# Routing tables of a mixture-of-experts kernel rebuilt: ranks, a scan, token numbers in the one-hots, and the last low parts on another engine

## The chip, the cores and the metric

The kernel runs on one core of a Trainium2 chip. Its time is the device time of one execution in microseconds (us). The engines run side by side and wait for each other by semaphores: TensorE (PE) multiplies, VectorE (DVE), ScalarE (ACT) and GpSimd (POOL) do the rest, SyncE (SP) issues plain DMAs. GpSimd issues the indirect DMAs that gather and scatter rows.

## The reference, cut to what matters

All is fp32; T = 2048 tokens of 512 numbers, 8 experts, 2 chosen for each token.

```python
x = x + xattn(ctx, ctx, mask, kpad, layernorm(x), Wq, bq, Wk, bk)   # softmax(scores * layernorm(x))
xn = layernorm(x).reshape(-1, 512)
shared = silu(xn @ shared_gate_w) * (xn @ shared_up_w) @ shared_down_w
logits = xn @ router_w                                # (2048, 8)
top_val, top_idx = top_k(logits, 2)
probs = zeros.at[arange(T)[:, None], top_idx].set(sigmoid(top_val))
for e in range(8):                                    # probs is 0 where e is not chosen
    gate, up = split((probs[:, e, None] * xn) @ gate_up_w[e], 2)
    shared += (silu(gate) * up) @ down_w[e]
out = x + shared
```

## The kernel before, in words

The tokens are 16 tiles of 128 (`TILES`). In a first phase (to about 122 us) each tile passes attention, normalisation, router logits and the shared expert. In a last phase (from about 153 us) come 39 routed jobs (`ROUTED`), numbered 16 to 54: each gathers 128 rows of one expert from memory (`gather`, `xg`), transposes them, multiplies by that expert's weights and adds the result to the output by an indirect DMA (`scatter`). Rows beyond a job's tokens go to a spare place. Jobs are sorted by expert.

Between the phases stands the routing, on which the change works. `fetch` copies logits from PSUM, first of 14 tiles (`FIRST`), then of the last two. `choose` finds a maximum by a chain: maximum, equality, index, one-hot `oh`, and the first choice masked out before the second. `ohs` is their sum. TensorE's `ranks` gives by matrix products with `ones` and `triangle` each choice's number within its expert. `count` turns them into jobs per expert (`ntile`, a running sum by three shifted additions) and `base`, `place_of_choice` into a `slot` for each of the 32 columns of choices, of which `job` and `row` are the high and low bits. `G` is the one-hot of the job, `OB` that of the row, in four parts that share two buffers. TensorE's `job_rows` multiplies them to a map job by row that holds a token number, in two halves (`R`: the token's number in its tile, and 128 times the tile, made by ScalarE from `G`), to be added. `jgather` and `jscatter` are the row numbers for the DMAs, `jexpert` the experts of the jobs, `jneed` how far each scatter waits for earlier ones.

Weights and activations are split in a high part and a low part (`gu_hi`, `gu_lo`; `x_hi`, `x_lo`), and three products stand for an fp32 one. Expert weights come in 27 chunks (`CHUNKS`): SyncE loads one into `stage`, ScalarE makes the high part, GpSimd the low part (`low_part`, `late_low`). The last six chunks come late, since their places hold other tensors in the first phase.

The order on each engine is the order in which the code is written; each engine has one queue, and nothing is moved by a scheduler. `then` makes VectorE wait for the end of its own instruction. `keep_busy` are transposes whose result is not used. On GpSimd a gather waits until `xg` is free (`h_s`), a scatter until y is there and until the three scatters before it are done, as far as they may touch the same rows; the first seven wait for all three.

## Time and profile before

| | before |
|---|---|
| median of 3 runs | 353.49 us (353.42 to 355.19) |
| profiled execution | 353.46 us |
| its span | 351.6 us |
| TensorE busy | 318.0 us, 90% |
| VectorE busy | 206.8 us, 59% |
| ScalarE busy | 181.0 us, 51% |
| GpSimd busy | 212.2 us, 60% |
| mean granted TensorE clock | 0.981 |
| moved by DMA | 50.60 MB, mean 144 GB/s |

Rows of the profile are of one execution; L numbers are lines of the kernel. Of each instruction it shows start and duration. Instructions of one engine overlap a little, so the distance of two starts is less than a duration where nothing is waited for. PE is TensorE's matrix product, PEld its weight load.

### The profile page before, as it was taken

Reading aid. Unit: us, or ns where it says so; the run is one execution under the profiler, and the core shown is the slowest. Engines: PE = TensorE matmul, PEld = TensorE weight load, DVE = VectorE, ACT = ScalarE, POOL = GpSimd, SP = SyncE. Lnnn points to the kernel's source line nnn. Section 1 sums busy time; section 2 is a strip of 40 time slices with the busy share of each in tenths; the row PEclk is TensorE's granted clock in tenths of the full one; section 3 lists DMA queues with packets and bytes.
Section 4 is the critical chain, followed back from the end, with each engine's and each line's share of the span. In section 5 each row is a group of like instructions: output and inputs, shape, how many; then the busy total and the mean of one; then the engine's idle time right before and its main releaser. Section 6 shows DMA issues by size and latency. Waiting matters only on the chain.

```text
span 351.6 us, 6597 instructions
## 1 busy us (share of the span) xinstructions
PE 318.0 (90%) x1677; PEld 222.4 (63%) x1677; DVE 206.8 (59%) x453; ACT 181.0 (51%) x409; POOL 212.2 (60%) x206
## 2 busy tenths in 40 slices
PE   2868999899999897879998989999999999999990
PEld 1334666676777666647766757777777777777760
DVE  0695888899998799834443444444444444445440
ACT  2578777767868745135544434444344444434430
POOL 0699999988686700393683666665465565555333
PEclk9989999999999999699999999999999999999998
DMA  7956678856755421281556486666666576565635
GB/s 175 320 216 230 213 239 241 245 204 209 236 159 187 170 92 7 66 292 38 90 97 115 70 170 99 109 110 118 117 122 108 88 128 108 115 123 100 113 45 75
DMA packets 29762, 50.60 MB, mean 144 GB/s; under 512 B 5472, under 2 KB 9312, under 8 KB 29728
## 3 DMA queue, kind: packets, MB, share of 16 engines
q0 software_dynamic: 9008, 21.66, 34.4%
q1 hardware_dynamic: 19232, 27.99, 24.7%
q10 hardware_dynamic: 1488, 0.54, 0.7%
q8 instruction: 16, 0.26, 0.3%
q14 instruction: 18, 0.15, 0.1%
HBM read 30.45 MB, written 19.73 MB: 143 GB/s over the span
## 4 chain that ended last, share of the span: by engine, by line
PE 60%; POOL 12%; DMA 10%; issue 9%; DVE 4%; SPq 2%; ACT 2%; POOLq 0%; DVEq 0%; ACTq 0%
PE bank L963 10%; PE bank L1007 10%; PE bank L968 8%; DMA out_rows<-y,jscatter 6%; PE bank L1028 4%; PE bank L1034 4%; PE bank L1031 4%; POOL gu_lo L362 4%; PE bank L1133 4%; PE bank L1016 2%; POOL dn_lo L362 2%; DMA xin<-in_x 2%; PE bank L926 2%; PE bank L985 2%; PE bank L935 2%
## 5 line engine op out<-in xcount | busy, mean ns | idle before, releaser
L442 POOL DMA_INDIRECT out_rows<-y,jscatter x39 | 61.9, 1587 | 74.1 <-DMA out_rows<-y,jscatter 52.1
L1007 PE MATMUL bank<-gu_hi,x_lo 128*128 (+1 forms) x220 | 72.8, 452 | 0.6 <-DVE x_lo L679 0.6
L963 PE MATMUL bank<-gu_hi,x_hi 128*128 (+1 forms) x220 | 61.6, 402 | 3.7 <-ACT x_hi L514 2.6
L423 POOL DMA_INDIRECT xg<-xn_rows,jgather x39 | 41.7, 1069 | 27.5 <-DVE jgather L839 15.3
L1007 PEld LDWEIGHTS bank<-gu_hi,x_lo 128*128 128x128 f32 x220 | 41.3, 189 | 18.0 <-issue 4.3
L878 DVE SCALAR_TENSOR_TENSOR h<-bank,xg,h 128x256 f32<-128x256 f32 x39 | 18.9, 484 | 56.0 <-ACT h L603 56.0
L522 ACT CAST h_hi<-bank 128x256 fp32r<-128x256 f32 x55 | 20.5, 374 | 60.7 <-PE bank L1016 57.0
L963 PEld LDWEIGHTS bank<-gu_hi,x_hi 128*128 128x128 f32 x220 | 40.0, 188 | 14.7 <-issue 2.8
L679 DVE TENSOR_TENSOR x_lo<-bank,x_hi 128x512 fp32r<-128x512 f32 x55 | 37.9, 690 | 19.0 <-ACT x_bf L515 18.6
L362 POOL TENSOR_TENSOR gu_lo<-stage,gu_hi 128x1024 bf16<-128x1024 f32 x18 | 43.4, 2410 | 5.6 <-ACT gu_hi L501 5.6
L603 ACT ACTIVATE h<-bank,xg 128x256 f32<-128x256 f32 x39 | 18.5, 474 | 50.0 <-PE bank L1007 26.4
L968 PE MATMUL bank<-gu_lo,x_bf 128*128 (+1 forms) x172 | 44.2, 379 | 0.0
L685 DVE TENSOR_TENSOR h_lo<-bank,h_hi 128x256 fp32r<-128x256 f32 x55 | 23.1, 420 | 32.9 <-ACT h_bf L523 32.8
L1034 PE MATMUL bank<-dn_hi,h_lo 128*128 (+1 forms) x86 | 35.5, 494 | 0.0
L514 ACT CAST x_hi<-bank 128x512 fp32r<-128x512 f32 x55 | 31.9, 581 | 6.3 <-PE bank L1133 4.3
L515 ACT CAST x_bf<-bank 128x512 bf16<-128x512 f32 x55 | 32.9, 598 | 0.0
L1028 PE MATMUL bank<-dn_hi,h_hi 128*128 (+1 forms) x86 | 30.8, 439 | 2.1 <-DVE x L699 1.0
L887 DVE COPY y<-bank 128x512 f32<-128x512 f32 x39 | 26.6, 681 | 1.3 <-PE bank L1034 1.3
L1031 PE MATMUL bank<-dn_lo,h_bf 128*128 (+1 forms) x86 | 26.5, 391 | 0.0
L1133 PE MATMUL bank<-ident,xg 128*128 128x128 f32 x156 | 23.5, 273 | 2.2 <-DMA xg<-xn_rows,jgather 2.2
L357 POOL TENSOR_TENSOR pen<-mask_pen,kpad_pen 128x512 bf16<-128x512 bf16 x16 | 18.6, 1160 | 10.1 <-DVE kpad_pen L705 10.0
L362 POOL TENSOR_TENSOR dn_lo<-stage,dn_hi 128x1024 bf16<-128x1024 f32 x9 | 21.9, 2438 | 4.5 <-ACT dn_hi L501 4.4
(145 smaller groups left out, 553.2 us busy)
## 6 DMA issues: line engine op xcount, KB each, us to landing
stage<-in_L_ffn_gate_up_w SPq DMA_DIRECT2D x16, 512.0 KB, 3.9
xin<-in_x SPq DMA_DIRECT2D x16, 256.0 KB, 4.4
xn_rows<-xn SPq DMA_DIRECT2D x16, 256.0 KB, 4.0
stage<-in_L_ffn_down_w SPq DMA_DIRECT2D x8, 512.0 KB, 3.7
out_rows<-x SPq DMA_DIRECT2D x16, 256.0 KB, 4.3
out_rows<-zeros POOLq DMA_DIRECT2D x1, 1024.0 KB, 5.0
ctx_in<-in_ctx SPq DMA_DIRECT2D x1, 768.0 KB, 8.8
xg<-xn_rows,jgather POOLq DMA_INDIRECT x39
```

Of the source, the lines that this page charges most:

```text
L362: g.tensor_tensor(third((gu_lo, dn_lo), c), stage[:, c % 3], third((gu_hi, dn_hi), c).bitcast(f32), ALU.subtract).then_inc(lo_s, 1)
L423: g.indirect_dma_start(out=xg[:, r, :], out_offset=None, in_=xn_dram, in_offset=bass.IndirectOffsetOnAxis(ap=jgather[:, n - TILES:n - TILE ...
L442: g.indirect_dma_start(out=out, out_offset=bass.IndirectOffsetOnAxis(ap=jscatter[:, n - TILES:n - TILES + 1], axis=0), in_=y[:, r, :], in_ ...
L515: a.copy(x_bf[:, n % TS], rows_T(n)).then_inc(xbf_s, 1)
L679: v.tensor_tensor(x_lo[:, n % TS], rows_T(n), x_hi[:, n % TS].bitcast(f32), ALU.subtract).then_inc(xlo_s, 1)
L963: tn.matmul(ps_g(n)[:], x_hi[:, n % TS, k, :], gu_hi[:, e, k, :], start=(k == 0), stop=False)
L968: tn.matmul(ps_g(n)[:], x_bf[:, n % TS, k, :], gu_lo[:, e, k, :], start=False, stop=False)
L1007: last = tn.matmul(ps_g(n)[:], x_lo[:, n % TS, k, :], gu_hi[:, e, k, :], start=False, stop=(k == KC - 1))
L1028: tn.matmul(ps_y(n)[:], h_hi[:, n % 2, c, :], dn_hi[:, e, c, :], start=(c == 0), stop=False)
L1031: tn.matmul(ps_y(n)[:], h_bf[:, n % 2, c, :], dn_lo[:, e, c, :], start=False, stop=False)
L1034: last = tn.matmul(ps_y(n)[:], h_lo[:, n % 2, c, :], dn_hi[:, e, c, :], start=False, stop=(c == IC - 1))
L1133: last = tn.transpose(ps_xT[n % 2][:, k * P:(k + 1) * P], xg[:, n % XS, k * P:(k + 1) * P], ident[:])
```

## The change

- `choose_both` finds both choices of the last two tiles by counting: a logit's rank is the number of logits that are larger, or as large and of a lower expert (`below`); rank 0 and 1 are the choices. The 14 tiles before keep the chain.
- The running sum in `count` is one `tensor_tensor_scan`.
- `OB` carries the token number: 32 instructions of 128 elements compare with the row and multiply by `tokens`, in fp16 and in a buffer of their own; `R`, `tok1` and ScalarE's multiplications and copy go. The map has one half, 39 columns, and `jgather` and `jscatter` read it from PSUM.
- `last_normal` moves ahead of `fetch`; `job_experts` moves behind the shared gates; the down product of tile 13 moves behind the map; `h_transpose` of tile 15 gets a PSUM bank of its own and moves ahead of the down product of tile 14.
- The low parts of chunks 24 to 26 are made by VectorE (`last_low`), one before the routed jobs and one in each of jobs 18 and 19.
- On GpSimd the gather runs five jobs ahead of the scatter, where it was four.

```diff
@@ -32,13 +32,14 @@
 READY = EARLY + 1
+LAST = CHUNKS - 3
 FIRST = TILES - LAG
@@ -373,9 +377,8 @@ (GpSimd)
             def late_low(c):
-                place, i = c // 3, c % 3
-                if i < 2:
-                    t = TILES - XS + 2 * (place - 7) + i
+                if c % 3 < 2:
+                    t = TILES - XS + c % 3
...
-            for c in range(READY, READY + 3):
+            for c in range(READY, LAST):
                 late_low(c)
...
+            gather(TILES + XS)
             for n in range(TILES, JOBS):
-                if n + XS < JOBS:
-                    gather(n + XS)
+                if n + XS + 1 < JOBS:
+                    gather(n + XS + 1)
                 scatter(n)
-                if n in (TILES + 1, TILES + 2):
-                    late_low(READY + 3 + n - TILES - 1)
@@ -586,15 +590,8 @@ (ScalarE)
-            act.wait_ge(G_s, 1)
-            for t in range(TILES):
-                last = a.mul(R[:].rearrange("p (k t) m j -> p k t m j", k=K)[:, :, t, 1, :],
-                             G[:].rearrange("p (k t) j -> p k t j", k=K)[:, :, t, :], float(P * t))
...
+            act.wait_ge(map_ps, 4)
             late_high(EARLY + 3)
-            act.wait_ge(map_ps, 4)
-            a.copy(amap[:].rearrange("p a j -> p (a j)"), ps_map).then_inc(map_s, 1)
@@ -768,11 +765,31 @@ (VectorE)
+            def choose_both(first, end):
+                n = end - first
+                src = lgs[:, first:end, :]
+                seen = src.unsqueeze(2).to_broadcast([P, n, E, E])
+                own = src.unsqueeze(3).to_broadcast([P, n, E, E])
+                v.tensor_tensor(larger[:], seen, own, ALU.is_gt)
+                then(v.tensor_tensor(as_large[:], seen, own, ALU.is_ge))
+                then(v.tensor_tensor(as_large[:], as_large[:], below[:].unsqueeze(1).to_broadcast([P, n, E, E]), ALU.mult))
+                then(v.tensor_tensor(larger[:], larger[:], as_large[:], ALU.max))
+                then(v.tensor_reduce(eq[:, first:end, :], larger[:], X, ALU.add))
+                v.tensor_scalar(ohs[:, (first + 1) * E:(end + 1) * E].rearrange("p (t e) -> p t e", e=E),
+                                eq[:, first:end, :], float(K), None, ALU.is_lt).then_inc(ohs_s, 1)
+                for k in range(K):
+                    v.tensor_scalar(oh[:, k].rearrange("p (t e) -> p t e", e=E)[:, first:end, :], eq[:, first:end, :],
+                                    float(k), None, ALU.is_equal).then_inc(oh_s, 1)
...
-                for i, d in enumerate((1, 2, 4)):
-                    then(v.tensor_tensor(ntile[i + 1][:, 4:], ntile[i][:, 4:], ntile[i][:, 4 - d:4 - d + E], ALU.add))
-                then(v.tensor_tensor(base[:], ntile[3][:, 4:], ntile[0][:, 4:], ALU.subtract))
+                then(v.tensor_tensor_scan(base[:], ones[:, 0:E], ntile[:, 3:3 + E], 0.0, ALU.mult, ALU.add))
...
-                dve.wait_ge(G_s, 1)
-                v.tensor_scalar(R[:, :, 0, :], G[:], tok1[:], None, ALU.mult).then_inc(R1_s, 1)
 
             def row_of_choice(part):
-                n = NC // 4
-                if part >= 2:
-                    dve.wait_ge(map_ps, part - 1)
                 dve.wait_ge(row_s, 1)
-                v.tensor_tensor(OB[part % 2][:], iotap[:].unsqueeze(1).to_broadcast([P, n, P]),
-                                wide(rowf[:, part * n:(part + 1) * n], [P, n, P]), ALU.is_equal).then_inc(OB_s, 1)
+                for i in range(part * NC // 4, (part + 1) * NC // 4):
+                    last = v.tensor_scalar(OB[:, i, :], iotap[:], rowf[:, i:i + 1], tokens[:, i:i + 1], ALU.is_equal, ALU.mult)
+                last.then_inc(OB_s, 1)
...
+            def rows_to_gather():
+                dve.wait_ge(map_ps, 4)
+                v.tensor_scalar(jgather[:], ps_map, -1.0, 0.0, ALU.add, ALU.max).then_inc(table_s, 1)
...
+            def last_low(c):
+                if c % 3 < 2:
+                    t = TILES - 2 + c % 3
+                    dve.wait_ge(st_xn[t % XS], stored_xn(t))
+                    dve.wait_ge(xT_ps, t + 1)
+                else:
+                    dve.wait_ge(max_s, TILES)
+                dve.wait_ge(hi_s, c + 1)
+                v.tensor_tensor(third((gu_lo, dn_lo), c), stage[:, c % 3], third((gu_hi, dn_hi), c).bitcast(f32),
+                                ALU.subtract).then_inc(lolast_s, 1)
+
+            last_normal()
+            x_low(TILES - 2)
             fetch(0, 0, FIRST)
-            x_low(TILES - 2)
-            last_normal()
             choose(0, 0, FIRST)
-            h_low(FIRST - 1)
             x_low(TILES - 1)
             choose(1, 0, FIRST)
+            clear_ends()
+            sum_of_choices(0, FIRST)
             fetch(1, FIRST, TILES)
-            choose(0, FIRST, TILES)
-            choose(1, FIRST, TILES)
-            chosen_sum()
+            choose_both(FIRST, TILES)
             weights_of_choices()
             count()
             place_of_choice()
             job_of_choice()
-            row_of_choice(0)
-            row_of_choice(1)
-            row_of_choice(2)
-            row_of_choice(3)
-            job_experts()
-            tables()
+            for part in range(4):
+                row_of_choice(part)
+            rows_to_gather()
+            h_low(FIRST - 1)
             gated_shared(TILES - 2)
+            rows_to_scatter()
             gated_shared(TILES - 1)
             y_shared(FIRST - 2)
+            job_experts()
             h_low(TILES - 2)
-            scatter_waits()
             y_shared(FIRST - 1)
             h_low(TILES - 1)
+            scatter_waits()
+            last_low(LAST)
             y_shared(TILES - 2)
             y_shared(TILES - 1)
...
                 if n > TILES:
                     h_low(n - 1)
+                if n in (TILES + 2, TILES + 3):
+                    last_low(LAST + n - TILES - 1)
                 gated(n)
@@ -1096,29 +1125,28 @@ (TensorE)
             h_transpose(FIRST - 1)
+            xn_transpose(TILES - 1)
             gate_up_high(TILES - 2, SHARED)
-            xn_transpose(TILES - 1)
...
             gate_up_high(TILES - 1, SHARED)
-            down(FIRST - 1, SHARED)
             pe.wait_ge(pexp_s, TILES)
             ranks()
             gate_up_low(TILES - 1, SHARED)
             gate_up_rest(TILES - 1, SHARED)
-            keep_busy(28)
-            pe.wait_ge(R1_s, 1)
+            keep_busy(20)
+            pe.wait_ge(G_s, 1)
             for part in range(4):
-                pe.wait_ge(R0_s, min(part + 1, 2))
                 job_rows(part)
-                keep_busy(4)
-            keep_busy(6)
+                keep_busy(5)
+            down(FIRST - 1, SHARED)
             h_transpose(TILES - 2)
+            pe.wait_ge(scatter_s, 1)
+            h_transpose(TILES - 1)
             down(TILES - 2, SHARED)
-            h_transpose(TILES - 1)
             down(TILES - 1, SHARED)
```

VectorE from the cast of `row` on, before. `OB` are the row one-hots, their number a buffer, `ecmp` to `jlow` the experts:

```order
L807 CAST rowf<-row 128x32 [waits dve_step]
L810 TENSOR_TENSOR G<-jobf,jcolb 128x1248
L813 TENSOR_SCALAR R<-G,tok_101 128x32x39 [waits G_s]
L820 TENSOR_TENSOR OB_91<-iotap,rowf 128x1024 [waits row_s]
L820 TENSOR_TENSOR OB_92<-iotap,rowf 128x1024 [waits row_s]
L820 TENSOR_TENSOR OB_91<-iotap,rowf 128x1024 [waits row_s,map_ps]
L820 TENSOR_TENSOR OB_92<-iotap,rowf 128x1024 [waits row_s,map_ps]
L824 TENSOR_TENSOR ecmp<-jcol,ntile_123 128x312
L826 TENSOR_REDUCE efl<-ecmp 128x39 [waits dve_step]
L827 TENSOR_SCALAR jexpert<-efl 128x39 [waits dve_step]
L828 TENSOR_SCALAR jlow<-jexpert 128x8 [waits dve_step]
L838 TENSOR_TENSOR tok<-amap 128x39 [waits map_s]
```

The same place now (the row of seven repeats three times more with its first):

```order
L823 CAST rowf<-row 128x32 [waits dve_step]
L826 TENSOR_TENSOR G<-jobf,jcolb 128x1248
L832 TENSOR_SCALAR OB<-iotap,rowf,tokens 128x128 [waits row_s]
L832 TENSOR_SCALAR OB<-iotap,rowf,tokens 128x128 x7
...
L851 TENSOR_SCALAR jgather<-bank 128x39 [waits map_ps]
L682 TENSOR_TENSOR h_lo<-bank,h_hi 128x256 [waits y_ps,hbf_s]
L687 SCALAR_TENSOR_TENSOR h<-h,bank 128x256 [waits act_s]
L690 SCALAR_TENSOR_TENSOR h<-bank,h 128x256 [waits sm_s]
L854 TENSOR_SCALAR hole<-bank 128x39
```

`R` and `tok` are gone, the four wide instructions have become 32 narrow ones, and the experts no longer stand ahead of `jgather`.

GpSimd from the low parts behind the first four gathers on, before:

```order
L362 TENSOR_TENSOR gu_lo<-stage,gu_hi 128x1024 [waits hi_s,xT_ps,st_xn1]
L362 TENSOR_TENSOR dn_lo<-stage,dn_hi 128x1024 [waits hi_s,max_s]
L362 TENSOR_TENSOR gu_lo<-stage,gu_hi 128x1024 [waits hi_s,xT_ps,st_xn2]
...
L442 DMA out_rows<-y,jscatter 2560x512 [waits y_s]
L423 DMA xg<-xn_rows,jgather 128x520 [waits h_s]
L442 DMA out_rows<-y,jscatter 2560x512 [waits add_y0,y_s]
L362 TENSOR_TENSOR gu_lo<-stage,gu_hi 128x1024 [waits hi_s,xT_ps,st_xn3]
L423 DMA xg<-xn_rows,jgather 128x520 [waits h_s]
L442 DMA out_rows<-y,jscatter 2560x512 [waits add_y0,add_y1,y_s]
```

The same place now:

```order
L366 TENSOR_TENSOR gu_lo<-stage,gu_hi 128x1024 [waits hi_s,xT_ps,st_xn1]
L366 TENSOR_TENSOR dn_lo<-stage,dn_hi 128x1024 [waits hi_s,max_s]
...
L428 DMA xg<-xn_rows,jgather 128x520 [waits h_s]
L447 DMA out_rows<-y,jscatter 2560x512 [waits y_s]
L428 DMA xg<-xn_rows,jgather 128x520 [waits h_s]
L447 DMA out_rows<-y,jscatter 2560x512 [waits add_y0,y_s]
L428 DMA xg<-xn_rows,jgather 128x520 [waits h_s]
L447 DMA out_rows<-y,jscatter 2560x512 [waits add_y0,add_y1,y_s]
```

Three low parts have left GpSimd's queue, and two gathers stand before the first scatter.

## Rows read from the trace of the kernel before

**Rows 1.** Waits, 108 to 160 us: us in total, times, longest

```profile
POOL xg L423 <- DVE jgather L839: 15.3, 1, 15.3
```

**Rows 2.** Windows of routing: stretch, length, busy times (instructions), granted clock, DMA

```profile
138.00:140.00 2.00, 0.92 (x12) 0.71 (x12) 2.00 (x3) 2.00 (x13) 0.00 (x0) 1.00 0.00 0
140.00:142.00 2.00, 1.79 (x21) 1.63 (x22) 2.00 (x3) 0.81 (x1) 0.00 (x0) 0.65 0.00 0
```

**Rows 3.** Timeline of VectorE, routing: start, duration, instruction

```profile
123.30 0.69 DVE L679 TENSOR_TENSOR x_lo<-bank,x_hi 128x512 fp32r<-128x512 f32 x1
123.90 0.54 DVE L782 TENSOR_SCALAR xn<-x,mv,rstd 128x512 f32<-128x512 f32 x1
...
128.66 0.17 DVE L755 COPY lgs<-bank 128x16 f32<-128x16 f32 x1
...
131.46 0.94 DVE L787 RECIPROCAL p<-p 128x128 f32<-128x128 f32 x1
132.46 0.29 DVE L791 TENSOR_TENSOR cmp<-bank,k 128x128 f32<-128x128 f32 x1
...
133.10 0.57 DVE L794 TENSOR_TENSOR ntile<-ntile 128x8 f32<-128x8 f32 x3
...
135.15 0.18 DVE L804 TENSOR_SCALAR job<-slot 128x32 int32<-128x32 int32 x1
135.25 0.17 DVE L805 TENSOR_SCALAR row<-slot 128x32 int32<-128x32 int32 x1
...
135.76 1.45 DVE L810 TENSOR_TENSOR G<-jobf,jcolb 128x1248 bf16<-128x1248 bf16 x1
137.25 0.55 DVE L813 TENSOR_SCALAR R<-G,tok 128x1248 bf16<-128x1248 bf16 x1
137.71 4.62 DVE L820 TENSOR_TENSOR OB<-iotap,rowf 128x1024 bf16<-128x1024 bf16 x4
...
143.99 0.18 DVE L839 TENSOR_SCALAR jgather<-tok 128x39 int32<-128x39 f32 x1
```

**Rows 4.** Timeline of TensorE, end of routing and first routed job

```profile
147.05 0.86 PE L1028 MATMUL bank<-dn_hi,h_hi 128*128 128x512 f32 x2 [1.04 <-DVE x L699]
...
149.44 0.63 PE L1016 MATMUL bank<-ident,h 128*128 128x128 f32 x2
...
153.55 1.18 PE L963 MATMUL bank<-gu_hi,x_hi 128*128 x4 [0.83 <-ACT x_hi L514]
```

**Rows 5.** Windows of the first routed job's wait and of three jobs

```profile
143.99:154.56 10.57, 7.58 (x32) 4.58 (x30) 7.05 (x21) 2.37 (x6) 8.44 (x6) 0.84 0.61 199
181.70:187.85 6.15, 5.13 (x26) 3.15 (x24) 2.55 (x5) 2.19 (x5) 2.67 (x2) 1.00 0.67 133
202.20:208.47 6.27, 4.96 (x26) 3.34 (x25) 2.22 (x5) 2.19 (x5) 5.11 (x4) 1.00 0.92 168
208.47:213.22 4.75, 4.75 (x26) 3.41 (x25) 2.19 (x5) 2.08 (x5) 1.58 (x2) 1.00 0.46 102
```

**Rows 6.** Timeline of TensorE, the transposes of job 27

```profile
206.60 0.66 PE L1133 MATMUL bank<-ident,xg 128*128 128x128 f32 x4 [1.30 <-DMA xg<-xn_rows,jgather]
```

**Rows 7.** Timeline of GpSimd

```profile
121.27 0.58 POOL L332 TENSOR_TENSOR rstd<-ve,mhalf 128x1 f32<-128x1 f32 x1
...
171.65 2.91 POOL L362 TENSOR_TENSOR gu_lo<-stage,gu_hi 128x1024 bf16<-128x1024 f32 x1
...
180.50 1.08 POOL L423 DMA_INDIRECT xg<-xn_rows,jgather  x1 [0.16 <-issue]
...
193.53 1.59 POOL L442 DMA_INDIRECT out_rows<-y,jscatter  x1 [2.64 <-issue]
...
199.18 1.59 POOL L442 DMA_INDIRECT out_rows<-y,jscatter  x1 [2.69 <-DVE y L887]
201.07 1.07 POOL L423 DMA_INDIRECT xg<-xn_rows,jgather  x1 [0.30 <-issue]
```

**Rows 8.** Waits, 160 to 212 us

```profile
DVE h L878 <- ACT h L603: 14.0, 10, 1.4
```

More of the change, by code:

```diff
@@ L145, in build @@
         jlow = new("jlow", [P, CAREFUL], i32)
-        tok1 = new("tok1", [P, 1])
         pidx = new("pidx", [P, ROUTED + 1])
@@ L161, in build @@
         row = new("row", [P, NC], i32)
-        rowf = new("rowf", [P, NC], bf16)
-        jobf = new("jobf", [P, NC], bf16)
-        jcolb = new("jcolb", [P, ROUTED], bf16)
-        ntile = [new(f"ntile{i}", [P, 4 + E]) for i in range(4)]
+        jobf = new("jobf", [P, NC], f16)
+        tokens = new("tokens", [P, NC])
+        below = new("below", [P, E, E])
+        jcolb = new("jcolb", [P, ROUTED], f16)
+        ntile = new("ntile", [P, 4 + E])
+        ends = new("ends", [P, E])
         base = new("base", [P, E])
@@ L405, in _ @@
                     iota(pidx[:], [[0, (ROUTED + 1) // XS], [P, XS]], T + 1, 1)
-                    for i in range(4):
-                        g.memset(ntile[i][:], 0.0)
+                    g.memset(ntile[:], 0.0)
+                    then(g.memset(below[:], 1.0))
+                    g.affine_select(out=below[:], in_=below[:], compare_op=ALU.is_gt, fill=0.0, base=0,
+                                    pattern=[[1, E], [-1, E]], channel_multiplier=0)
                 if s == 7:
@@ L1049, in job_rows @@
                 for i in range(part * n, (part + 1) * n):
-                    last = tn.matmul(ps_map, OB[part % 2][:, i - part * n, :], R[:, i].rearrange("p m j -> p (m j)"),
-                                     start=(i == 0), stop=(i == NC - 1))
+                    last = tn.matmul(ps_map, OB[:, i, :], G[:, i], start=(i == 0), stop=(i == NC - 1))
                 last.then_inc(map_ps, 1)
```

77 lines of the change are left out of this document (41 added, 36 removed).

## The prediction, on record before the changed kernel ran

> **What bounds the kernel now.** I read five views, in this order: the totals per engine and the waits, the chain of waits, the timeline of each engine from 120 to 160 us, and last the windows and the timeline of the routed jobs. The totals name TensorE (90% busy), but an average says nothing of the place that is changed, so I looked for where TensorE does no useful work. There are two such places.
>
> The first is the routing step, 122 to 154 us. GpSimd waits 15.3 us in one piece for the gather table `jgather` [rows 1]. VectorE runs from the second `fetch` at 128.66 us to `jgather` at 143.99 us without a gap [rows 3], so VectorE sets this stretch; TensorE fills it with `keep_busy` transposes. TensorE's clock falls to its lower level, 1.2 GHz, within it: 0.65 is granted on the mean of 140 to 142 us, after 2 us in which the engine was busy 0.92 us [rows 2]. The first routed job's gate product starts at 153.55 us [rows 4].
>
> The second is in the routed jobs. A job costs TensorE 4.75 us when nothing stalls, and 6.15 and 6.27 us in two jobs [rows 5]; in the second of them it waits 1.30 us for gathered rows [rows 6]. These are 1.40 + 1.52 = 2.9 us in all. The cause stands on GpSimd: the gather at 180.50 us comes behind two low parts of some 2.9 us each, and the one at 201.07 us behind scatters that leave one every 5.65 us, since each of the first seven waits for all before it [rows 7].
>
> **The change, part by part.** I take start-to-start times on VectorE, for they add up; durations overlap by some 0.09 us.
>
> Order at the start of the routing. `last_normal` needs only GpSimd's `rstd`, which ends at 121.27 + 0.58 = 121.85 us [rows 7], but stands behind `fetch` and `x_low` and starts at 123.90 us [rows 3]. Now it starts at 121.9, `x_low` ends at 123.05, and TensorE's transposes of tile 15, which wait for both, start at 123.1, earlier than `xn` had been begun. VectorE's list from there is 0.46 (xn) + 0.60 (x_low) + 0.34 (fetch) + 6 x 0.305 (first choice, 112 elements, by `cmp` on 128: 0.29 and a gap of 0.03) + 0.60 (x_low) + 5 x 0.305 (second choice) + some 0.4 (two memsets, sum of choices) = 5.8: the second fetch moves from 128.66 to 127.7 us. TensorE's logits of tile 15 end at 127.5 by the same count, so neither waits long.
>
> Late choices by ranks. Removed: 11 instructions of 0.17 to 0.25 us and the sum, 128.87 to 131.46 = 2.6 us. Added up to `ohs`: one pair without a wait (0.2), four more on 128 elements at 0.32 as `cmp`, one of 0.2 on 16: 1.6 us, so `ohs` is there at 129.5. The ranks on TensorE (0.8 us) no longer come behind a down product and end at 130.3, but VectorE still has two `oh` writes and the reciprocal of 0.94 us [rows 3] to do: it starts the count at 130.65 instead of 132.46 us. Gain so far 1.8 us.
>
> The scan. Three additions (0.57 in one row, 0.61 with their gaps) and a subtraction of 0.2 become one scan of 8 elements. No row shows a scan. Bounds: 0.20 (a plain instruction of that size) and 0.57 (the three that it replaces). I take 0.2, since 8 elements are fewer than any size at which elements count here: gain 0.6, total 2.4. `G` starts at 133.35 us instead of 135.76 [rows 3].
>
> The row one-hots. Removed: R on VectorE, 0.46, and 16 multiplications on ScalarE that lie beside it. The four `OB` instructions take 4.62 us; in their place stand 32 of 128 fp16 elements, each with two operands read per partition (row and token). This is the largest unknown. The full price of an element is 1.04 ns, from G and `cmp`: (1.45 - 0.29) / (1248 - 128) [rows 3]. `row` starts 0.10 us after `job`, with 32 elements and no such operand. R has one such operand and 1248 16-bit elements in 0.46 us, so an element costs it about a quarter, 0.26 ns, and some 0.135 us are fixed. `xn` has two and 512 fp32 elements; it takes 0.54 less the overlap, 0.46, which is under 512 full prices; at half a price an element it is 0.27 and 0.19 fixed. So each operand seems to add some 0.05, and one of the new instructions takes 0.19 + 128 x 0.26 ns = 0.225, all 32 take 7.2 us. This is 2.6 us more than the four. Lower bound: 0.10 + 0.033, 4.3 us. Upper bound: 0.19 + 0.133 at the full price, which the old `OB` pays (1024 elements in 1.15), 10.3 us. I take 7.2, by xn, the only row with two such operands. So `OB` runs from 134.75 to 142.0, where the old ended at 142.33: the head start of 2.9 us (R's half included) is nearly spent.
>
> The Trainium skill speaks to this place (VectorE: DVE Perf Modes, section "The TRN2 errata — SBUF-src ops pay a fixed extra latency per instruction"): many small tiles pay a fixed cost each, and its table has 58 cycles plus the elements over the mode's factor. An estimate by that table is 0.094 us an instruction at factor 4 and 3.0 us for 32, and the sum would end at 344.5. The rows of R and xn lie 0.08 and 0.13 us over the same formula, so the trace agrees in kind and not in size.
>
> One map. TensorE's products have 39 columns instead of 78; they end some 0.8 us after the last `OB` at the low clock. ScalarE's copy `amap` (0.22) and the addition `tok` (0.24) go, and VectorE reads the map from PSUM: `jgather` at 142.85 instead of 143.99 us, gain 1.15. Gathers start as much earlier, which is long enough before their first reader.
>
> From there to the first routed job VectorE has one unbroken list. Before, from `jgather` to the end of `x_low` of job 16, it was busy 7.05 us of 10.57 [rows 5]. To this list come the experts from ahead of `jgather` (five small instructions, 1.5), `h_low` of tile 13 (0.34) and a low part (1.14): 10.0 us. It ends at 152.9. TensorE has the maps' end at 142.8, five transposes 0.8, the moved down product (2.4 us at the low clock, as that at 147.05 us took until 149.44 [rows 4]), two transposes, then at 147.0 the down product of tile 14, which waits for its `h_lo`: VectorE has `job_experts` ahead of that now, so it comes at 148.0 and the product ends near 148.9. The one of tile 15 ends at 150.2; transposes and ScalarE's copies take 1.4 as before: the gate product of job 16 starts at 151.7 instead of 153.55 us. **Gain 1.9 us.** The down product that went from ahead of the ranks comes back here.
>
> Low parts on VectorE. The three last go from GpSimd to VectorE. One costs 1.14 us there: `x_low`'s 0.60 for 512 elements [rows 3], and 512 more at 1.04 ns. Two stand in jobs 18 and 19 between `h_low` and `gated`: there VectorE waits for ScalarE's silu, 14.0 us in 10 jobs [rows 8], 1.4 each, and is busy only 2.19 of 4.75 us [rows 5], so they are hidden; uncovered they would cost 2.3. ScalarE's high parts come in the job before each, so none waits long.
>
> Gathers one deeper. On GpSimd `gather(n + 5)` stands ahead of `scatter(n)`. It waits for the gated product of job n + 1, which VectorE ends before it copies y of job n, for which the scatter waits: nothing queued behind it is late. The scatters' cadence of 5.65 us stays, starting at 163.3; so gather 23 is issued behind the second scatter at 170.9 and gather 27 behind the sixth at 193.3 us. Their readers come at 183 and 202, and 5.5 us are needed, from the gather at 201.07 to its reader at 206.60 [rows 6, 7]. **Both stalls go: gain 2.9 us.** After the seventh scatter the waits are shorter, and I see nothing that takes the stalls' place.
>
> GpSimd's tables `tokens` and `below` in place of smaller ones I cost at nothing: they stand beside TensorE's work at 62 to 69 us, and were they not covered they would cost a few tenths.
>
> **The sum.** The profiled execution took 353.46 us, its span 351.6; the median of the runs is 353.49, so the sum carries over. 353.46 - 1.9 - 2.9 = 348.7 us.
>
> **The rivals.**
> - Cheap one-hots. Reading the two operands overlaps with the instruction before, and 32 take 4.5 us or less (0.14 each, R's fixed part with nothing more). For it: `row` behind `job`, 0.10. Against it: xn. The start gains 2.7 more: 346.0. The Trainium skill's table named above goes beyond this, to 344.5; a third of this case's chance would be its.
> - One-hots at the full price of an element, 10.3 us: 348.7 + 3.1 = 351.8. For it: the old OB ran so. Against it: R, a 16-bit instruction of the same kind, does not.
> - The gather stalls stay, because the scatters' cadence and not the gather's place sets them, or because the deeper gather queues behind a scatter's transfer: 348.7 + 2.9 = 351.6. For it: the scatters do fall behind the jobs. Against it: 9 us of room by the sum.
> - Slower than before. Each one-hot instruction waits for the end of the one before, as the chained ones do (a duration of 0.27 + 0.133 at the full price, and a gap of 0.035: 0.44 us), 14.1 us in all: 348.7 + 6.9 = 355.6. It decides from 0.375 us an instruction on, where 4.8 us are lost. Against it: `row` overlaps `job`, and they are of this kind.
>
> **How the numbers follow.** Chances: forecast 0.50, cheap one-hots 0.18, stalls stay 0.14, full price 0.09, slower 0.09. A measurement tells a change from none at about 0.5%, 1.8 us, so "faster" is below 351.7. It holds the first two, most of the third (0.10): 0.77 with a little off the forecast's tail. Same: the rest of the third and the fourth, 0.14. Slower 0.09. The range reaches from the cheap case with some margin to the case of the full price: 345.3 to 351.8.
>
> **What would show it.** Right: `OB` starts 0.2 to 0.25 us apart, 32 of them over some 7.2 us; second fetch near 127.7, `G` near 133.4, `jgather` near 142.9, gate product of job 16 near 151.7; every job from 17 on at 4.75 us; low parts on VectorE of 1.2 us with no TensorE wait on `h` in jobs 18 and 19. Wrong: `OB` much under or over 7 us; a TensorE wait for `xg` between 180 and 210 us; TensorE waiting for VectorE's `x_lo` of job 16, which I have 0.5 us before it is needed; or a longer stretch at the low clock.

## The result: the time after, and the profile of the changed kernel

| | before | after |
|---|---|---|
| median of 15 runs | 354.50 us | 356.41 us |
| ratio after/before, 95% interval | | 1.0058 [1.0036, 1.0080] |
| profiled execution, its span | 353.46, 351.6 us | 355.48, 353.7 us |
| mean granted clock | | 0.976 |

The prediction was 348.7 us with a range of 345.3 to 351.8. The time is outside it and on the other side: the change costs about 1.9 us.

Stages are compared from a common mark, since two executions of one kernel differ in the phase ahead of the routing: the last phase-1 gated product on VectorE starts at 121.16 us in the profile of before, at 123.86 us in a second profile of the same kernel (experiment 9), and at 123.26 us after. From that mark:

| us from the mark | second `fetch` | `G` | `jgather` | gate product of job 16 | of job 17 | of job 54 |
|---|---|---|---|---|---|---|
| before | 7.50 | 14.60 | 22.83 | 32.39 | 36.70 | 215.52 |
| before, second profile | 7.50 | 14.60 | 22.80 | 31.48 | 35.77 | 213.91 |
| after | 6.47 | 11.97 | 21.03 | 29.79 | **39.87** | 215.80 |

After is ahead at each mark up to job 16. Between the gate products of job 16 and job 17 it loses all of that: 10.08 us where before took 4.31. It catches up later, since no gather stalls a job: 175.93 us for the 37 intervals from job 17 to job 54 (4.755 each) against 178.82 and 178.14.

The timeline of VectorE in the kernel after, routing (start, duration, instruction; these answer to [rows 3]):

```profile
129.73 0.17 DVE L752 COPY lgs<-bank 128x16 f32<-128x16 f32 x1
...
133.18 0.17 DVE L810 TENSOR_TENSOR_SCAN base<-ones,ntile 128x8 f32<-128x8 bf16 x1
...
135.23 1.45 DVE L826 TENSOR_TENSOR G<-jobf,jcolb 128x1248 f16<-128x1248 f16 x1
136.60 7.22 DVE L832 TENSOR_SCALAR OB<-iotap,rowf,tokens 128x128 f16<-128x128 f16 x32
144.29 0.20 DVE L851 TENSOR_SCALAR jgather<-bank 128x39 int32<-128x39 f32 x1 [0.47 <-PE bank L1080]
```

The 32 one-hots take 7.22 us, 0.226 each, as estimated. The same engine further on:

```profile
149.93 0.42 DVE L682 TENSOR_TENSOR h_lo<-bank,h_hi 128x256 fp32r<-128x256 f32 x1
150.26 5.21 DVE L845 TENSOR_TENSOR other<-efl 128x38 f32<-128x38 f32 x1
155.51 0.20 DVE L846 SCALAR_TENSOR_TENSOR jneed<-other,turns 128x38 int32<-128x38 f32 x1
155.63 0.19 DVE L845 TENSOR_TENSOR other<-efl 128x37 f32<-128x37 f32 x1
...
156.30 1.22 DVE L866 TENSOR_TENSOR gu_lo<-stage,gu_hi 128x1024 bf16<-128x1024 f32 x1
157.44 1.28 DVE L696 TENSOR_TENSOR x<-bank,x 128x512 f32<-128x512 f32 x2
158.64 0.68 DVE L676 TENSOR_TENSOR x_lo<-bank,x_hi 128x512 fp32r<-128x512 f32 x1
```

A comparison of 38 elements takes 5.21 us. The same line with 37 elements, 5 us later, takes 0.19. Work for one element less can't make this difference: the first instruction is held. What GpSimd does in that time is in the timeline of GpSimd in the kernel after (same columns; in square brackets the idle time ahead and what ended it):

```profile
149.68 1.01 POOL L428 DMA_INDIRECT xg<-xn_rows,jgather  x1 [0.30 <-issue]
150.72 2.36 POOL L366 TENSOR_TENSOR gu_lo<-stage,gu_hi 128x1024 bf16<-128x1024 f32 x1
153.03 2.38 POOL L366 TENSOR_TENSOR dn_lo<-stage,dn_hi 128x1024 bf16<-128x1024 f32 x1
163.58 1.03 POOL L428 DMA_INDIRECT xg<-xn_rows,jgather  x1 [8.17 <-DVE h L903]
```

GpSimd's two low parts end at 155.41, VectorE's comparison at 155.47. The timeline of TensorE in the kernel after shows the price (it answers to [rows 4]):

```profile
153.05 1.18 PE L990 MATMUL bank<-gu_hi,x_hi 128*128 x4 [0.83 <-ACT x_hi L518]
154.08 1.04 PE L995 MATMUL bank<-gu_lo,x_bf 128*128 x4
159.38 2.07 PE L1034 MATMUL bank<-gu_hi,x_lo 128*128 x4 [4.26 <-DVE x_lo L676]
```

TensorE waits 4.26 us for `x_lo` of job 16, and then these four products take 2.07 us, where later jobs have 0.93 (the chain of waits, below). The windows of the kernel after, of job 16's whole interval, of those four products, and of a later job (columns as in [rows 5]):

```profile
153.05:163.13 10.08, 4.99 (x16) 3.03 (x17) 6.65 (x11) 1.55 (x4) 2.36 (x2) 0.83 0.44 146
159.38:161.45 2.07, 2.07 (x5) 1.58 (x6) 0.00 (x0) 0.00 (x0) 0.00 (x0) 0.50 1.06 286
187.00:191.75 4.75, 4.75 (x25) 3.35 (x24) 2.19 (x5) 2.08 (x5) 2.66 (x2) 1.00 0.51 82
```

TensorE is idle in half of the interval. The granted clock is 0.50, the 1.2 GHz level, throughout the products that follow the idle 4.26 us, and back at 1.00 in the later job. The chain of waits of the kernel after runs through the comparison (start, us, what):

```profile
150.35 5.14 DVE other L845
...
159.38 2.07 PE bank L1034 x4
...
165.41 0.93 PE bank L1034 x4
```

Measured from the second profile of before, the balance is: start of job 16, -1.69 us (31.48 to 29.79); interval of job 16, +5.79 (4.29 to 10.08); later jobs, -2.21 (178.14 to 175.93). The sum is +1.9 us, the difference of the medians. From the first profile it is -2.60 + 5.77 - 2.89 = +0.3; the rest of the 2.1 us between the two spans is the 2.10 us at the mark, less 0.3 us behind job 54. The mark is not the change's doing: over the fourteen profiles of this study it lies at 121.16 to 124.77 us in the six that have the old routing and at 121.53 to 124.97 us in the eight that have the new one.

### The profile page after: what moved, and what is told of

Same layout as the page of the kernel before. It is cut to its first block, busy times and chain, and to the rows that moved or that the text cites. A ratio compares the mean times of both kernels' runs of the same rounds, so it can differ in the third digit from the quotient of the medians.

```text
span 353.7 us, 6606 instructions
## 1 busy us (share of the span) xinstructions
PE 318.4 (90%) x1667; PEld 221.7 (63%) x1667; DVE 216.2 (61%) x477; ACT 178.2 (50%) x392; POOL 205.6 (58%) x202
## 4 chain that ended last, share of the span: by engine, by line
PE 70%; POOL 9%; DVE 9%; issue 5%; DMA 4%; ACT 2%; DVEq 0%; SPq 0%; POOLq 0%; ACTq 0%
PE bank L990 13%; PE bank L1034 12%; PE bank L995 9%; PE bank L1058 5%; PE bank L1064 5%; PE bank L1161 5%; PE bank L1061 5%; POOL gu_lo L366 3%; PE bank L1046 3%; DMA out_rows<-y,jscatter 3%; PE bank L953 3%; PE bank L1012 2%; DVE OB L832 2%; POOL dn_lo L366 2%; PE bank L962 2%
## 5 line engine op out<-in xcount | busy, mean ns | idle before, releaser
L990 PE MATMUL bank<-gu_hi,x_hi 128*128 (+1 forms) x220 | 62.5, 406 | 3.4 <-ACT x_hi L518 2.5
L366 POOL TENSOR_TENSOR gu_lo<-stage,gu_hi 128x1024 bf16<-128x1024 f32 x16 | 38.1, 2382 | 7.1 <-ACT gu_hi L505 7.1
L995 PEld LDWEIGHTS bank<-gu_lo,x_bf 128*128 128x128 bf16 x172 | 16.4, 98 | 11.4 <-issue 0.8
```

The lines of the kernel that those rows point to most:

```text
L366: g.tensor_tensor(third((gu_lo, dn_lo), c), stage[:, c % 3], third((gu_hi, dn_hi), c).bitcast(f32), ALU.subtract).then_inc(lo_s, 1)
L990: tn.matmul(ps_g(n)[:], x_hi[:, n % TS, k, :], gu_hi[:, e, k, :], start=(k == 0), stop=False)
L995: tn.matmul(ps_g(n)[:], x_bf[:, n % TS, k, :], gu_lo[:, e, k, :], start=False, stop=False)
```

## The experiments

My theory after the result (from here on "port"): a VectorE instruction with two SBUF inputs is held while GpSimd works on SBUF. The first rival, called "wait" below: the comparison waits for a semaphore or for its input, or something in the scatter tables' own place or data is slow, whatever GpSimd does. The Trainium skill has a rule for it (SBUF — State Buffer, section "Who interferes with whom"): a VectorE instruction with two SBUF inputs contends with a GpSimd instruction that reads SBUF and not with one that only writes, and whichever comes first has the port for its whole instruction. The trace agrees so far: low parts read two SBUF tensors, and VectorE ended 0.06 us behind them. I had not weighed this rule in the prediction.

**1. The tables earlier.** The changed kernel, with `scatter_waits` right behind the experts.

```diff
             job_experts()
+            scatter_waits()
             h_low(TILES - 2)
             y_shared(FIRST - 1)
             h_low(TILES - 1)
-            scatter_waits()
             last_low(LAST)
```

> The changed kernel with scatter_waits moved from behind h_low of tile 15 to right behind job_experts; the low part of chunk 24 stays where it was. Port theory (a VectorE instruction with two SBUF tensor inputs does not get through while GpSimd runs its two low parts): the first comparison into other takes 0.19 us instead of 5.21, but the low part on VectorE, which now meets GpSimd's, is held until GpSimd ends at about 155.4, so the rest product of job 16 starts at 157 to 158.5 instead of 159.38 and the kernel is 1 to 2 us faster than the changed one, about 1.000 of before. Wait theory (the comparison waits for a semaphore or for its input, whatever GpSimd does): it is either long again in the new place, or the hold vanishes altogether and the kernel is 5.4 us faster than the changed one.

Measured: 357.58 us, ratio 1.0080 [1.0051, 1.0109]. A miss. The timelines of VectorE, GpSimd and TensorE in this kernel, one behind the other:

```profile
149.95 5.34 DVE L846 SCALAR_TENSOR_TENSOR jneed<-other,turns 128x36 int32<-128x36 f32 x1
149.54 1.01 POOL L428 DMA_INDIRECT xg<-xn_rows,jgather  x1 [0.30 <-issue]
150.58 2.35 POOL L366 TENSOR_TENSOR gu_lo<-stage,gu_hi 128x1024 bf16<-128x1024 f32 x1
152.88 2.34 POOL L366 TENSOR_TENSOR dn_lo<-stage,dn_hi 128x1024 bf16<-128x1024 f32 x1
155.67 1.22 PE L1064 MATMUL bank<-dn_hi,h_lo 128*128 128x512 f32 x2 [6.95 <-DVE h_lo L682]
```

The hold moved to another instruction, the last `jneed`, and ends with GpSimd again. So it is not the first comparison that is slow; it is whatever of this kind meets the low parts. The move was too small to get clear of them, and what was now behind it, `h_lo` of tile 14, is needed sooner than `x_lo`: TensorE waits 6.95 us.

**2. VectorE's low part later too.** As 1, with `last_low(LAST)` behind the call `x_low(TILES)`, which is job 16's.

```diff
-            last_low(LAST)
...
             x_low(TILES)
+            last_low(LAST)
```

> As the run before, and the low part of chunk 24 moved behind x_low of job 16. Port theory: both holds leave the path; the low part is held until GpSimd ends near 155.4, under the wait for silu of job 16, x_low of job 16 ends near 153.5 and the gap from the gate product of job 16 to that of job 17 goes from 10.1 to about 4.5 us; 5.4 us faster than the changed kernel, ratio to before about 0.99. Wait theory: the same as for the run before. If the head of the kernel (2.1 us later in the changed kernel's profile than in that of before) is a cost of the change and not of the execution, the ratio is 0.995 and the profile has tile 11's gate product at 111.2, not at 109.1 us.

Measured: 358.76 us, 1.0102 [1.0060, 1.0144]; the last `jneed` is held 5.33 us. A miss for the same reason: `scatter_waits` stands where it stood in experiment 1, and moving other work changes nothing in its hold.

**3. GpSimd only writes.** The changed kernel; GpSimd's two late low parts (chunks 22 and 23) become zeros, so these two low parts are left out of the result.

```diff
-                low_part(c)
+                if c >= READY:
+                    pool.wait_ge(hi_s, c + 1)
+                    g.memset(third((gu_lo, dn_lo), c), 0.0).then_inc(lo_s, 1)
+                else:
+                    low_part(c)
```

> The changed kernel, but GpSimd fills the low parts of chunks 22 and 23 with zeros (a memset, no SBUF input) instead of computing them, so these low parts are left out of the products. Port theory: GpSimd reads nothing, the comparison into other takes 0.19 us and the low part on VectorE 1.2 us at the old places, 5.4 us faster than the changed kernel. Wait theory: the comparison still takes 5 us.

Measured in one run: 351.48 us, and the interval of job 16 is 4.29 us where the changed kernel has 10.08. The timelines of GpSimd and VectorE in this kernel:

```profile
152.42 0.98 POOL L388 MEMSET gu_lo<- 128x1024 bf16 x1
153.31 0.98 POOL L388 MEMSET dn_lo<- 128x1024 bf16 x1
152.00 0.19 DVE L849 TENSOR_TENSOR other<-efl 128x38 f32<-128x38 f32 x1
153.01 1.22 DVE L870 TENSOR_TENSOR gu_lo<-stage,gu_hi 128x1024 bf16<-128x1024 f32 x1
```

No instruction is held, though VectorE's own low part, with two SBUF inputs, runs beside both memsets. Place and data of the comparison are as in the changed kernel, so the rival falls.

**4. What helped, alone.** The kernel before with the two low parts of chunks 25 and 26 on VectorE in jobs 18 and 19, and the gathers one deeper; its routing is untouched.

```diff
+            gather(TILES + XS)
...
-                if n + XS < JOBS:
-                    gather(n + XS)
+                if n + XS + 1 < JOBS:
+                    gather(n + XS + 1)
...
-                if n in (TILES + 1, TILES + 2):
-                    late_low(READY + 3 + n - TILES - 1)
...
+                if n in (TILES + 2, TILES + 3):
+                    last_low(LAST + n - TILES - 2)
```

> The kernel before with the two changes in the routed jobs alone: the low parts of chunks 25 and 26 on VectorE in jobs 18 and 19, and the gather one job deeper. My forecast for these two: both gather stalls go and nothing else changes, 2.9 us faster than before, ratio 0.992, every job from 17 on at 4.75 us. Rival: the scatters' cadence keeps the stalls, ratio 1.000. Port rival: VectorE's low parts in jobs 18 and 19 are held by GpSimd's indirect DMAs, or hold them, and a job there is longer than 4.75 us.

Measured: 351.58 us, 0.9918 [0.9891, 0.9945], as forecast. The 2.9 us are real and were covered by the hold.

**5. Both out of the low parts' way.** The changed kernel, with `last_low(24)` behind `x_low(16)` and `scatter_waits` behind `x_low(17)`.

```diff
-            scatter_waits()
-            last_low(LAST)
...
             x_low(TILES)
+            last_low(LAST)
...
                 if n + 1 < JOBS:
                     x_low(n + 1)
+                if n == TILES:
+                    scatter_waits()
```

> The changed kernel with the low part of chunk 24 moved behind x_low of job 16 and scatter_waits behind x_low of job 17, so that from h_low of tile 15 to x_low of job 16 VectorE has only instructions with one input in PSUM. Port theory, as the runs so far leave it (a VectorE instruction with two SBUF inputs that begins up to half a microsecond before or during GpSimd's low parts is held until both have ended, one with an input in PSUM is not): no hold on the path, rest product of job 16 within 1.7 to 2 us of its gate product, the low part on VectorE held until GpSimd ends and then done before silu of job 16; 5.4 us faster than the changed kernel in the profile's stretches, about 351, ratio 0.985 to 0.99. Rival: x_low or y_shared is held in their place, ratio 1.00 or more.

Measured: 351.09 us, 0.9887 [0.9851, 0.9922]. The timelines of VectorE and GpSimd in this kernel:

```profile
152.87 0.69 DVE L696 TENSOR_TENSOR x<-bank,x 128x512 f32<-128x512 f32 x1 [0.87 <-PE bank L1065]
154.41 0.69 DVE L676 TENSOR_TENSOR x_lo<-bank,x_hi 128x512 fp32r<-128x512 f32 x1 [0.85 <-ACT x_bf L519]
155.02 2.56 DVE L866 TENSOR_TENSOR gu_lo<-stage,gu_hi 128x1024 bf16<-128x1024 f32 x1
157.88 0.48 DVE L901 SCALAR_TENSOR_TENSOR h<-bank,xg,h 128x256 f32<-128x256 f32 x1 [0.29 <-ACT h L600]
151.77 2.39 POOL L366 TENSOR_TENSOR gu_lo<-stage,gu_hi 128x1024 bf16<-128x1024 f32 x1
154.09 2.40 POOL L366 TENSOR_TENSOR dn_lo<-stage,dn_hi 128x1024 bf16<-128x1024 f32 x1
```

Two things stand here. `x` and `x_lo`, each with one input from PSUM and one from SBUF, run at their usual 0.69 us within GpSimd's low parts. And VectorE's low part takes 2.56 us: it is held until GpSimd ends at 156.49, then does its 1.1 us. It ends 0.3 us before `gated` of job 16 can start, so the hold is there and costs nothing. Only two calls stand elsewhere than in the changed kernel: the ratio falls from 1.0058 to 0.9887, some 6 us, and the interval of job 16 is 4.31 us again.

**6. Wide one-hots.** Kernel 5 with `OB` by four wide fp16 comparisons as before; the token numbers come in by ScalarE, which multiplies `G` (16 instructions into `GT`).

```diff
-                    last = v.tensor_scalar(OB[:, i, :], iotap[:], rowf[:, i:i + 1], tokens[:, i:i + 1], ALU.is_equal, ALU.mult)
+                v.tensor_tensor(OB[:, part * n:(part + 1) * n, :], iotap[:].unsqueeze(1).to_broadcast([P, n, P]),
+                                wide(rowf[:, part * n:(part + 1) * n], [P, n, P]), ALU.is_equal).then_inc(OB_s, 1)
...
+                last = a.mul(GT[...], G[...], tokens[:, t:t + 1])
```

> As the run before, but the row one-hots by four wide comparisons as in the kernel before (fp16), and the token numbers multiplied into G by ScalarE, 16 instructions beside them. If the 32 narrow instructions are the price that was measured (7.22 us against 4.62), jgather comes 2.6 us earlier behind G and the kernel is 2 to 2.6 us faster than the run before, ratio about 0.98. Rival: TensorE's products and ScalarE's multiplications become the limit, and less than 1 us comes out.

Measured: 349.76 us, 0.9848 [0.9808, 0.9888]. The median is 1.3 us below that of kernel 5 where 2 or more were expected, but the two intervals overlap, and the traces show less: from the mark, `jgather` comes at 20.95 us against 21.12, and the gate product of job 16 at 29.69 against 29.86. So the wide one-hots are worth some 0.2 us here, and the remainder is not shown. Its timelines of VectorE and ScalarE:

```profile
137.35 4.62 DVE L839 TENSOR_TENSOR OB<-iotap,rowf 128x1024 f16<-128x1024 f16 x4
144.94 0.20 DVE L858 TENSOR_SCALAR jgather<-bank 128x39 int32<-128x39 f32 x1 [2.96 <-PE bank L1088]
137.47 4.11 ACT L596 ACTIVATE GT<-G,tokens 128x78 f16<-128x78 f16 x16 [0.50 <-DVE G L833]
```

The one-hots are 2.6 us shorter, but VectorE then waits 2.96 us for TensorE. ScalarE needs 0.26 us a multiplication by a value per partition; before, with a constant, bf16 and another layout of the output, it was 0.165 (16 in 2.63 us). And TensorE has `keep_busy` transposes between the map's products, at a granted clock of 0.50. The windows of this kernel:

```profile
142.00:144.00 2.00, 2.00 (x20) 1.94 (x17) 0.00 (x0) 0.00 (x0) 0.00 (x0) 0.50 0.04 8
144.00:146.00 2.00, 2.00 (x17) 1.94 (x17) 1.03 (x4) 1.05 (x1) 0.00 (x0) 0.50 0.00 0
```

VectorE has nothing at all from 142 to 144 us and TensorE is full, so TensorE bounds this stretch.

**7. The hold put into the kernel before.** `scatter_waits` moved behind `y_shared(14)`, nothing else.

```diff
             h_low(TILES - 2)
-            scatter_waits()
             y_shared(FIRST - 1)
             h_low(TILES - 1)
             y_shared(TILES - 2)
+            scatter_waits()
             y_shared(TILES - 1)
```

> The kernel before with one move: scatter_waits from behind h_low of tile 14 to behind y_shared of tile 14, where GpSimd computes its three low parts. Port theory: the first comparison there takes until GpSimd's last low part ends, some 5 us, x_low of job 16 comes 3 to 5 us later, and the kernel is 3 to 5 us slower than before, ratio 1.008 to 1.014. Rival (the hold needs something that only the changed kernel has): 1.000.

Measured: 362.17 us, 1.0211 [1.0164, 1.0258], more than expected. The timeline of VectorE and of GpSimd in this kernel:

```profile
153.88 5.43 DVE L832 TENSOR_TENSOR other<-efl 128x38 f32<-128x38 f32 x1
156.92 2.33 POOL L362 TENSOR_TENSOR gu_lo<-stage,gu_hi 128x1024 bf16<-128x1024 f32 x1
```

The hold is made at will in a kernel with the old routing, and ends with the last low part, at 159.25 us. The interval of job 16 is 8.85 us where before has 4.31, and that of job 17 is 7.08 where before has 4.84: its products ran at a granted clock of 0.55 (164.48 to 169.75 us). This second loss was not in the expectation. The later intervals are as before, with the gather stalls at jobs 22 and 26 (6.00 and 5.90 us). In the kernel before itself nothing of the kind met. Its timelines of VectorE and GpSimd at that place:

```profile
147.15 0.19 DVE L832 TENSOR_TENSOR other<-efl 128x38 f32<-128x38 f32 x1
...
151.13 0.68 DVE L699 TENSOR_TENSOR x<-bank,x 128x512 f32<-128x512 f32 x1
149.37 1.01 POOL L423 DMA_INDIRECT xg<-xn_rows,jgather  x1 [0.30 <-issue]
150.41 2.39 POOL L362 TENSOR_TENSOR gu_lo<-stage,gu_hi 128x1024 bf16<-128x1024 f32 x1
```

The comparison is over before the first low part, and beside the low parts VectorE has only instructions with an input from PSUM.

**8. One SBUF input on GpSimd.** As 3, with a plain copy in place of the zeros; the low parts of chunks 22 and 23 hold other numbers.

```diff
+                    g.tensor_copy(third((gu_lo, dn_lo), c), stage[:, c % 3]).then_inc(lo_s, 1)
```

> The changed kernel, but on GpSimd the low parts of chunks 22 and 23 are plain copies of the staged weights in bf16 (one SBUF input), so these low parts are wrong numbers. If two tensor inputs on GpSimd are what holds VectorE, the comparison into other takes 0.19 us as behind the memset; if any read of SBUF by GpSimd does, it is held for as long as the two copies run.

Measured in one run: 350.38 us, which can't be set against the 351.48 of experiment 3, since its mark lies 3.4 us earlier (121.53 against 124.97 us). The interval of job 16 is 6.19 us against 4.29 there. The timelines of VectorE and GpSimd in this kernel:

```profile
148.64 2.55 DVE L849 TENSOR_TENSOR other<-efl 128x38 f32<-128x38 f32 x1
149.09 1.04 POOL L388 CAST gu_lo<-stage 128x1024 bf16<-128x1024 f32 x1
150.08 1.04 POOL L388 CAST dn_lo<-stage 128x1024 bf16<-128x1024 f32 x1
```

Copies hold it too, to within 0.07 us of their end at 151.12. The length of the hold is that of GpSimd's instructions: 2.55 us with these, 5.21 with the low parts, none with memsets.

**9. The kernel before once more**, unchanged, for a second profile.

> The kernel before, unchanged, for a second profile of it. In the first, the gate product of tile 12 starts at 109.12 us; in the changed kernel's it does at 111.21. If this is the spread of the head from execution to execution, a second profile of before has it anywhere from 109 to 113 us; if it is a cost of the change, the second has 109.1 again.

Measured: 354.13 us, span 352.3. Its mark lies 2.7 us later than in the first profile, and it gains most of that back behind it. Absolute times of the start can't be compared to better than that; those from the mark agree to 0.03 us up to `jgather`, and to 0.9 us at job 16. The 0.9 us are TensorE's clock: the down product of tile 14 starts 25.9 us from the mark in both profiles, and takes 2.39 us to the next start at a granted clock of 0.58 in the first (147.05 to 149.44 us) and 1.45 us at 1.00 in the second (149.72 to 151.17). The kernel is the same, so it can run at either level there.

**10. No transposes between the map's products.** Kernel 6, with eight transposes behind the first of the four groups and five behind the last, in place of five behind each.

```diff
+                if part == 1:
+                    keep_busy(8)
                 pe.wait_ge(GT_s, min(part + 1, 2))
                 job_rows(part)
-                keep_busy(5)
+            keep_busy(5)
```

> The kernel with four wide one-hots and ScalarE's multiplications (e6), with no unused transposes between the four groups of map products (eight stand between the first and the wait for ScalarE's second half). In e6 the last group of products came 2.96 us after VectorE had the one-hots, behind ten transposes at the lower clock and ScalarE's second half. Transposes as the limit: jgather comes 1 to 1.9 us earlier behind G than in e6 (8.95 us) and the kernel is 1 to 1.9 us faster than e6. ScalarE as the limit or a lower clock for longer as the price: less than 0.5 us.

Measured: **347.94 us, 0.9822 [0.9792, 0.9853]**, the fastest version of the study, below both kernels, and 1.8 us below kernel 6. The two were not timed side by side; from the mark the gate product of job 16 comes at 27.53 us here and at 29.69 in kernel 6, 2.2 us earlier. The timelines of TensorE and VectorE in this kernel:

```profile
142.19 0.98 PE L1088 MATMUL bank<-GT,OB 128*128 128x39 f16 x24
143.21 0.20 DVE L858 TENSOR_SCALAR jgather<-bank 128x39 int32<-128x39 f32 x1 [0.68 <-PE bank L1088]
```

VectorE waits 0.68 us for the map instead of 2.96, and `G` to `jgather` takes 6.67 us instead of 8.95. The transposes that bridge a wait stand in the way once the wait is gone.

**11. The deeper gather alone** on the kernel before (first two pieces of the diff of 4).

> The kernel before with the gather one job deeper alone; all low parts stay on GpSimd. If the place of the gather in front of the scatter is what removes the stalls of 6.15 and 6.27 us, both jobs take 4.75 us and the kernel is 2.9 us faster, ratio 0.992. If the two low parts on GpSimd in jobs 17 and 18 caused the first of them, one stall of about 1.4 us stays, ratio 0.996.

Measured: 351.89 us, 0.9927 [0.9900, 0.9953]. Job 17 takes 4.83 us (4.84 in the kernel before), and no later job over 4.76. The 37 intervals sum to 175.79 us, those of kernel 4 to 175.75, so this is all of kernel 4's gain.

**12. The low parts alone** on the kernel before (the rest of the diff of 4).

> The kernel before with the low parts of chunks 25 and 26 on VectorE alone; the gather stays four jobs ahead. If GpSimd's low parts delayed the gathers, the first stall (6.15 us) goes and perhaps the second; ratio 0.992 to 0.996. If only the depth counts, both stay, ratio 1.000.

Measured: 354.43 us, 0.9997 [0.9969, 1.0024]. The stall of 6.15 us at job 22 is gone (4.75), but others stand in its place: intervals of 5.03, 5.55 and 5.65 us at jobs 24 to 26. The 37 intervals sum to 177.82 us, where the two profiles of before have 178.82 and 178.14. The scatters still leave one every 5.5 to 6.1 us from 165.85 to 200.35 us, and each gather stands behind one of them. So the low parts on GpSimd make one gather later than it need be, and the cadence of the scatters makes the gathers late as a whole.

## Why the prediction was wrong, point by point

- Order at the start of the routing: the second fetch 0.96 us earlier was forecast, 1.03 measured. Right.
- Ranks and the scan: `G` 2.4 us earlier was forecast, 2.63 measured. The scan of 8 elements takes 0.17 us, 0.21 to the next start, which is the lower bound, and gave the 0.6 us that were counted; the 0.2 us more come from the choices. Right.
- One-hots: 7.2 us forecast, 7.22 measured, which leaves out three rivals at once (cheap, full price, each waiting for the one before). Right.
- One map: `jgather` 1.15 us earlier was forecast, 1.80 measured. Of the 0.65 us more, 0.23 are `G`'s, and 0.38 come since `jgather` starts 0.47 us behind the last one-hot where I had 0.85.
- Gate product of job 16: gain 1.9 forecast, 2.60 measured against the first profile and 1.69 against the second, in which TensorE's clock is at the level that the changed kernel has there (experiment 9). Right. The moved down product was counted at 2.4 us, at the low clock; it took 1.46 (144.60 to 146.06 us) at a granted clock of 1.00, and nothing hung on it, since the next one waited for VectorE.
- **The step that failed** is "From there to the first routed job VectorE has one unbroken list ... 10.0 us. It ends at 152.9", 0.5 us before `x_lo` of job 16 is needed. The list took 15.03 us (144.29 to 159.32). Without the 5.02 us by which the comparison exceeds its 0.19 it is 10.0: each instruction was counted rightly, at its duration in the kernel before, where `scatter_waits` ran at 147.15 to 148.3 us, before GpSimd's first low part. The later place and GpSimd's low part at 150.72 us were both readable; I summed one engine's list as if no other engine could lengthen it. Experiments 3, 5, 7 and 8 show the cause from four sides: taken away on GpSimd, moved on VectorE, made in the kernel before, and shortened with GpSimd's instructions.
- Its price: 5.8 us in the interval of job 16, of which 4.26 us are TensorE's wait, 1.15 the same four products at the low clock (2.07 against 0.92 before), and most of the rest the transposes behind them (1.05 us against 0.60).
- Low parts on VectorE in jobs 18 and 19 hidden: right, at 1.22 us each where I had 1.14. They meet only gathers and scatters on GpSimd, which did not hold them (the first stands at 170.35 us within a scatter's record). The second, from 175.10 us, may have lengthened a scatter: that of 175.93 us took 1.86 us, where the ones around it have 1.57 to 1.64, and TensorE didn't wait for it.
- Deeper gather: 2.9 us forecast, 2.89 (2.21 by the second profile) measured. Right in size. Of its cause I had named two, the low parts ahead of the gather at 180.50 us and the scatters' cadence [rows 7]; the first explains at most the first stall, as experiments 11 and 12 show: the low parts' move alone removes that one and brings no gain, since others come in its place, and depth alone removes them all.
- The rival "slower" was there for a wrong reason, the price of a one-hot. What I listed as a sign of error, TensorE waiting for `x_lo` of job 16, is what came.

Open: why executions differ by up to 3.8 us at the mark, and why TensorE's clock is low before job 16 in one profile of before and high in the other. Not tried: the one-hots in their old form inside the changed kernel without the other edits of experiment 6.

## What to carry to other kernels

When an instruction moves on VectorE, look at what GpSimd runs at its new time, not only at what its own engine does: with two SBUF inputs it waited here, each time the two met, until the end of GpSimd's whole run of low parts or copies, and its usual duration says nothing. Put such instructions where their hold is covered by a wait that exists anyway, and leave in the critical place those that read PSUM. When a gain is missing, test the parts of a change alone: here one edit of a few lines was worth 0.7%, and the place of two calls 1.7%. And ask what bounds the stretch once a part of it is shorter: 2.6 us of one-hots gave 0.2 us, until the unused transposes behind them were moved too.

## What the runs showed of the hardware that I had not expected

- A held VectorE instruction stays held across GpSimd instructions that follow each other without a gap: 5.21 us over two low parts, 5.43 over what was left of three (experiment 7), 2.55 over two copies. The Trainium skill (SBUF — State Buffer, section "SBUF: two separate sides") says that the one that starts first has the shared port pair for the whole instruction and the other is blocked. The trace agrees on the block; it differs in that the waiting engine gets no turn between two instructions, and in that the held one can be recorded as starting before: 150.26 against 150.72 us after, 149.95 against 150.58 in experiment 1. In experiment 1 the comparison at 149.72 us, 0.86 us ahead of GpSimd's record, was not held. Since a comparison of 0.19 us would have ended before GpSimd's recorded start, either GpSimd takes its inputs before its record starts, or VectorE's record starts before it reads; this stays open.
- For instructions with two SBUF inputs, of what GpSimd ran only the low parts and the copies held them; memsets (0.98 us each), gathers and scatters (1.0 to 2.0 us) did not. The VectorE instructions `x` and `x_lo`, with one input in PSUM, ran at 0.69 us throughout.
- One instruction may be held by a gather. `jlow`, a VectorE instruction of 8 int32 elements with one SBUF input, takes 0.43 to 0.45 us in all eight profiles with the new routing, where it starts within the third gather's record and ends 0.02 to 0.04 us before that record does (148.92 us in the kernel after); it takes 0.17 us in all six with the old routing, where no gather runs. In experiments 1 and 2 the comparison right behind `jlow` ends together with it, after 0.36 and 0.35 us. Whether the gather is the cause was not tested.
- A VectorE comparison of 128 fp16 elements with two values read per partition takes 0.226 us start to start (32 in 7.22). ScalarE's multiplication of 78 elements took 0.165 us with a constant and 0.26 with a value per partition; the type and the layout of the output differ too, so the step is not shown to be the operand's alone.
